# Row maxima half a unit ahead, and both batches as one row of units

## The chip, the cores and the metric

The kernel runs on one core of a Trainium2 chip. The metric is the device time of one execution in microseconds (us). Three runs of the kernel before took 4086.3, 4100.18 and 4105.85 us; the median is 4100.18.

The engines are named as in the profile: PE is TensorE (PEld its weight loads), DVE is VectorE, ACT is ScalarE, POOL is GpSimd, SP is SyncE, which issues the transfers.

## What is computed

One layer: attention with one key and value head for 32 query heads, ALiBi bias and causal mask, then layer norm, then a feed-forward product with a routed low-rank part, and a second norm. x is 2 x 2048 x 1024 in float32.

```python
q = (x @ Wq).reshape(b, s, 32, 32)
k, v = x @ Wkv          # one head of 32 each
scores = einsum('bqhd,bkd->bhqk', q, k) * scale + slopes * (kpos - qpos)
attn = softmax(where(causal, scores, -inf), axis=-1)
x = layernorm(x + einsum('bhqk,bkd->bqhd', attn, v) @ Wo)
x = layernorm(x + x @ W.T + b + lora_of_chosen_rank(x))
```

## The kernel before

Attention is written for 2 batches, each of 4 segments of 512 queries. A segment s has 8 units, each of 4 heads (64 units in all, numbered 0 to 63 here; units 0 to 7 are segment 0 of the first batch). A unit takes its 512 queries against 4(s+1) key tiles of 128. Its steps:

- X (once a segment): the 512 rows of x are turned by TensorE in 8 parts (`turn_x`, line 652), split into a high part by ScalarE (`split_x`, line 454) and a low part by VectorE (line 542). KV: projection of keys and values, 24 products into ps_m, taken by VectorE (`take_kv`, lines 550 to 556). VT: the values are turned (line 673).
- Q: 8 parts of three products (lines 656 to 658) into ps_m for the unit after next; QE: taken from there head by head by ScalarE and VectorE (`take_q`, lines 466 and 567). WS: the next weights, loaded by SP into wq_raw, are split by ScalarE and POOL (lines 459 and 418).
- A: one chunk of scores, 128 queries against up to 512 keys, for the row maximum alone: TensorE into one of the three banks ps_a (line 692, with the mask 695), maximum by VectorE (line 574). The next unit has 16(s+1) of them.
- CV and CT: VectorE reduces the maxima (line 579), forms the shift (line 581), TensorE turns it into ps_m (line 700), VectorE copies it (line 585) and SP writes it into the last row of the query stack, where the next unit's first S waits for it.
- S: the scores of one key tile and one head, 128 keys by 512 queries, into one of two banks ps_s (line 756, mask 759), and the exponential by ScalarE (line 494). Such an S is a slot; a unit has 16(s+1) slots, four to a key tile.
- PV: probabilities times values of one key tile, SM: the same with ones for the row sums (line 779, four heads at a time, two passes each). In segments 1 to 3 POOL adds the probabilities of two tiles (ADD, line 437) and one SP takes the sum of both. OE: ScalarE copies both results; R: reciprocals by VectorE in 4 parts (line 592), the product by POOL (line 444), then the store.

`plan_step` writes the order of a unit's slots out for every engine: S, then what is put in that slot. Chunks A of unit g+1 go evenly into all but the last 7 slots (6 in segment 0); CV follows, CT two slots later. X, KV, VT, Q and QE follow one another from slot 1 on; X, KV and VT stand in the last unit but one of a segment. WS comes behind QE, in segment 0 in the last slot. PV and SM or SP go behind the second score of the next key tile. Every step waits on counting semaphores; a chunk A waits for the maximum three chunks before it.

`walk` runs each batch on its own: a prologue (X, KV, VT, Q, A for the first unit, Q for the second) in front of segment 0, then the units. SP loads wkv, then at 13 us x and wq_raw. The turned x goes into ps_m, one bank, save in the prologue (two banks of ps_a). The feed-forward stage begins when all of attention is through.

## Time and profile before

| | us |
|---|---|
| median of three runs | 4100.18 |
| the profiled execution's own time | 4086.85 |
| its span, first to last instruction | 4085.0 |
| attention, to the end of unit 63 | 3178.4 |
| feed-forward stage | 906.6 |
| PE busy in the span | 3766.8 (92%) |
| DVE, ACT, POOL busy | 2474.2 (61%), 1925.0 (47%), 1360.6 (33%) |
| PE's mean granted clock, of full | 0.959 |

Busy time counts an instruction from start to end. PE's matmuls are pipelined and their ends are modelled, so a busy PE may also be waiting. A unit is measured here from its first S to the next unit's first S. A wait in the timeline is shown in brackets: idle time of the engine, and what ended it.

### The profile page before, as it was taken

Reading aid. Unit: us, or ns where it says so; the run is one execution under the profiler, and the core shown is the slowest. Engines: PE = TensorE matmul, PEld = TensorE weight load, DVE = VectorE, ACT = ScalarE, POOL = GpSimd, SP = SyncE. Lnnn points to the kernel's source line nnn. Section 1 sums busy time; section 2 is a strip of 40 time slices with the busy share of each in tenths; the row PEclk is TensorE's granted clock in tenths of the full one; section 3 lists DMA queues with packets and bytes.
Section 4 is the critical chain, followed back from the end, with each engine's and each line's share of the span. In section 5 each row is a group of like instructions: output and inputs, shape, how many; then the busy total and the mean of one; then the engine's idle time right before and its main releaser. Section 6 shows DMA issues by size and latency. Waiting matters only on the chain. (4 is left out here: it accounts for less than half of the span.)

```text
span 4085.0 us, 56649 instructions
## 1 busy us (share of the span) xinstructions
PE 3766.8 (92%) x22065; PEld 2354.1 (58%) x22065; DVE 2474.2 (61%) x4462; ACT 1925.0 (47%) x3253; POOL 1360.6 (33%) x420
## 2 busy tenths in 40 slices
PE   5989989999999997888999999999998599999998
PEld 3555555555454543555555554544443488888887
DVE  4557767776767672555776777676764344444444
ACT  2435655665666664344665666566666211111110
POOL 1113434444445453112433444455555100000000
PEclk8879999999999998888999999999999799999999
DMA  2111110000000001211111000000000412111111
GB/s 71 40 53 32 32 42 22 22 22 22 14 19 14 19 6 34 60 37 45 32 30 45 19 22 22 14 22 13 20 14 3 145 62 62 61 57 57 57 60 52
DMA packets 158918, 150.73 MB, mean 37 GB/s; under 512 B 8388, under 2 KB 141508, under 8 KB 156584
## 3 DMA queue, kind: packets, MB, share of 16 engines
q1 hardware_dynamic: 158696, 147.70, 12.4%
q8 instruction: 148, 2.42, 0.2%
q14 instruction: 74, 0.61, 0.0%
HBM read 96.75 MB, written 33.62 MB: 32 GB/s over the span
## 5 line engine op out<-in xcount | busy, mean ns | idle before, releaser
L494 ACT ACTIVATE prob<-ps_s,alibi 128x512 f32<-128x512 f32 (+3 forms) x2560 | 1521.6, 623 | 1110.5 <-PE ps_s L756 545.6
L574 DVE TENSOR_REDUCE mxp<-ps_a 128x1 f32<-128x512 f32 (+3 forms) x2560 | 1457.8, 605 | 800.7 <-PE ps_a L695 418.4
L437 POOL TENSOR_TENSOR prob<-prob 128x2048 f32<-128x2048 f32 (+1 forms) x240 | 1044.4, 4351 | 1126.5 <-ACT prob L494 1126.5
L756 PE MATMUL ps_s<-qst,kexp 97*128 97x512 f32 (+3 forms) x2560 | 1092.3, 437 | 74.5 <-ACT prob L494 55.1
L692 PE MATMUL ps_a<-kmax,qst 97*128 97x512 f32 (+3 forms) x2560 | 956.1, 399 | 34.3 <-DVE mxp L574 17.3
L756 PEld LDWEIGHTS ps_s<-qst,kexp 97*128 97x128 f32 x2560 | 492.3, 194 | 727.6 <-ACT prob L494 425.1
L779 PE MATMUL ps_o<-prob,val 128*32 128x512 f32 (+3 forms) x5120 | 612.2, 551 | 7.7 <-ACT prob L494 7.7
L692 PEld LDWEIGHTS ps_a<-kmax,qst 97*128 97x128 f32 x2560 | 504.3, 198 | 116.7 <-DVE mxp L574 59.5
L779 PE MATMUL ps_sum<-prob,ones 128*32 128x512 f32 (+3 forms) x3200 | 361.4, 525 | 0.0
L965 POOL TENSOR_TENSOR hb_sb<-h_sb,bias_b 128x1024 f32<-128x1024 f32 x32 | 76.8, 2401 | 791.9 <-DVE z_sb L1109 732.2
L592 DVE RECIPROCAL r_sb<-s_sb 128x128 f32<-128x128 f32 x256 | 233.4, 928 | 113.8 <-ACT s_sb L500 113.1
L995 ACT ACTIVATE root<-var 128x1 f32<-128x1 f32 x64 | 13.0, 203 | 604.6 <-DVE var L1054 604.6
L418 POOL TENSOR_TENSOR wql<-wq_raw,wqh 128x1024 fp32r<-128x1024 f32 x65 | 154.4, 2375 | 396.3 <-ACT wqh L459 390.1
L1166 PE MATMUL ps_z<-wth,hth 128*128 128x364 f32 x768 | 254.8, 332 | 5.3 <-DVE htl L1121 5.3
L1168 PE MATMUL ps_z<-wtl,hth 128*128 128x364 f32 x768 | 252.9, 329 | 0.0
L1170 PE MATMUL ps_z<-wth,htl 128*128 128x364 f32 x768 | 252.8, 329 | 0.0
L695 PE MATMUL ps_a<-maskb,identb 128*128 128x128 bf16 x1024 | 242.5, 238 | 0.0
L759 PE MATMUL ps_s<-maskt,identb 128*128 128x128 bf16 x1024 | 239.6, 238 | 0.0
L656 PE MATMUL ps_m<-xh,wqh 128*128 128x512 f32 x512 | 225.1, 440 | 6.9 <-POOL wql L418 4.7
L567 DVE SCALAR_TENSOR_TENSOR qst<-ps_m,qst 32x512 fp32r<-32x512 f32 x256 | 176.1, 688 | 80.7 <-ACT qst L466 76.7
L657 PE MATMUL ps_m<-xl,wqh 128*128 128x512 f32 x512 | 213.8, 418 | 0.0
L658 PE MATMUL ps_m<-xh,wql 128*128 128x512 f32 x512 | 211.9, 414 | 0.0
(148 smaller groups left out, 3709.3 us busy)
## 6 DMA issues: line engine op xcount, KB each, us to landing
wq_raw<-in_L_attn_Wq SPq DMA_DIRECT2D x65, 512.0 KB, 4.0
xs<-in_L_attn_hidden_states SPq DMA_DIRECT2D x9, 2048.0 KB, 8.7
qst<-qst SPq DMA_DIRECT2D x64, 256.0 KB
att_scratch<-at_sb SPq DMA_DIRECT2D x64, 256.0 KB, 2.4
at_raw<-att_scratch SPq DMA_DIRECT2D x32, 512.0 KB, 5.3
x_sb<-in_L_attn_hidden_states SPq DMA_DIRECT2D x32, 512.0 KB, 4.3
out<-z_sb SPq DMA_DIRECT2D x32, 512.0 KB, 3.2
z_sb<-in_L_attn_Wo SPq DMA_DIRECT2D x4, 512.0 KB, 5.1
```

The source lines that it names most:

```text
L437: nc.gpsimd.tensor_tensor(even[:, :, c1:], even[:, :, c1:], odd[:, :, c1:], ALU.add).then_inc(pair_done, 1)
L494: nc.scalar.activation(prob[slot][:, h, c0:], ps_s[bank][:, c0:], ACT.Exp, bias=alibi_of(u, h, k - QT * s)).then_inc(e_done, 1)
L574: nc.vector.tensor_reduce(mxp[:, h * QT + t, c:c + 1], ps_a[bank][:, 0:cols], AX.X, ALU.max).then_inc(a_done, 1)
L592: nc.vector.reciprocal(r_sb[:, cols], s_sb[:, cols]).then_inc(r_done, 1)
L692: last = nc.tensor.matmul(ps[:, 0:cols], qst[buf][0:KR, h, t * P:(t + 1) * P], kmax[0:KR, c * QB:c * QB + cols], start=True, stop=c < s)
L695: last = nc.tensor.matmul(ps[:, cols - P:cols], identb[:], maskb[:], start=False, stop=True)
L756: last = nc.tensor.matmul(ps_s[bank][:, c0:], kexp[0:KR, k * P:(k + 1) * P], qst[buf][0:KR, h, c0:], start=True, stop=not diagonal)
L759: last = nc.tensor.matmul(ps_s[bank][:, c0:c0 + P], identb[:], maskt[:], start=False, stop=True)
L779: last = nc.tensor.matmul(ps[h * DH:(h + 1) * DH, c0:], weights, prob[slot][:, h, c0:], start=k == 0, stop=k == ktiles(s) - 1)
L1166: nc.tensor.matmul(ps, hth[:, c], wth[:, c, piece(p)], start=c == 0, stop=False, skip_group_check=True)
L1168: nc.tensor.matmul(ps, hth[:, c], wtl[:, c, piece(p)], start=False, stop=False, skip_group_check=True)
L1170: last = nc.tensor.matmul(ps, htl[:, c], wth[:, c, piece(p)], start=False, stop=False, skip_group_check=True)
```

## The change

The 64 units of both batches are one row; there is no second prologue. Keys and values stand in a ring of five segments, so that the first segment of the second batch can be prepared while the first batch still runs. The position row of kmax is written for each segment by VectorE.

The chunks A for unit g+1 end about halfway through unit g (A_END), CV follows at once and CT some slots later (CT_AT); in the rest of unit g stand the first chunks of unit g+2 (8, 13, 23 or 27 of them, none where unit g+2 has only 16). X, KV and VT go into the third unit from a segment's end. Each step has a table of places by segment.

The three banks ps_a are one ring: chunks, turned x and the turned maxima all take the next bank, and the counter a_done counts all three. The maxima themselves are turned, and VectorE makes the shift from the turned ones in one operation with a table `base` that is computed at the start. The shift operation of line 581 is gone.

In segments 2 and 3 the row sums (SM, SP) go behind the fourth score of a key tile (SM_AT), PV behind the second. WS in segment 0 is at slot 5. SP loads x first, then the weights; ScalarE waits for the bias table only before its first exponential.

The core of the diff ("..." marks what is left out):

```diff
--- before.py
+++ after.py
...
+SEGS = B * NSEG
+UNITS = SEGS * HG
+RING = NSEG + 1
...
+def ring(sg):
+    return sg % RING * QB
+def key_tile(g, k):
+    return (seg_of(g) // NSEG * NSEG + k // QT) % RING * QT + k % QT
...
-Q_SPACE = 0.5
-X_SPACE = (1, 1.5, 2.5, 2.5)
-RECIP_AT = ((2, 4, 6, 8, 9), (5, 19, 28, 29, 30), (14, 26, 44, 45, 46), (20, 36, 60, 61, 62))
...
+CHUNKS_AHEAD = (8, 13, 23, 27)
+A_END = (9, 17, 25, 33)
+A_FROM = (11, 18, 26, 34)
+Q_AT = ((0, 0.5), (0, 1), (0, 1.25), (1, 1.5))
+QE_AT = ((3, 1), (7, 2), (9, 3), (11, 5))
+CT_AT = (11, 18, 30, 38)
+X_AT = ((7, 0.5), (9, 1.25), (19, 2), (22, 3))
+KV_AT = (11, 25, 35, 46)
+VT_AT = (17, 27, 40, 47)
+PV_AT = (1, 1, 1, 1)
+SM_AT = (1, 1, 3, 3)
+WS_AT = (5, 17, 27, 33)
+RECIP_AT = ((0, 2, 3, 8, 11), (6, 16, 25, 29, 30), (22, 27, 44, 45, 46), (20, 36, 60, 61, 62))
+def chunks_ahead(g):
+    if g < 2:
+        return 0
+    return min(CHUNKS_AHEAD[seg_of(g - 2) % NSEG], len(a_chunks(g)) - GH * QT)
+def prepares(g):
+    return g % HG == HG - 3 and seg_of(g) + 1 < SEGS
...
+def plan_unit(g):
+    s = seg_of(g) % NSEG
+    n = ktiles(g)
     slots = n * GH
-    chunks = a_chunks(sa) if has_a else []
-    a_slots = slots - (7 if s else 6)
     at = {}
-    for i, x in enumerate(chunks):
-        at.setdefault(i * a_slots // len(chunks), []).append(("A", x))
-    if has_a:
-        at.setdefault(a_slots, []).append(("CV", 0))
-        at.setdefault(a_slots + 2, []).append(("CT", 0))
-    space = X_SPACE[s]
-    misc = [(space, ("X", j)) for j in range(DC)] + [(1, ("KV", 0)), (space, ("VT", 0))] if prep else []
-    if has_q:
-        misc += [(1 if s else Q_SPACE, ("Q", j)) for j in range(DC)]
-        misc += [(min(s + 1, 3), ("QE", h)) for h in range(GH)]
-    place = 1.0
-    for width, x in misc:
-        at.setdefault(min(a_slots - 1, int(place)), []).append(x)
-        place += width
-    if has_q:
-        at.setdefault(min(a_slots - 1, int(place)) if s else slots - 1, []).append(("WS", 0))
+    def put(slot, what, arg):
+        at.setdefault(min(slots - 1, int(slot)), []).append((what, arg))
+    if g + 1 < UNITS:
+        first = chunks_ahead(g + 1)
+        rest = a_chunks(g + 1)[first:]
+        for i, x in enumerate(rest):
+            put(i * A_END[s] / len(rest), "A", (g + 1, first + i, x))
+        put(A_END[s], "CV", 0)
+    if g + 2 < UNITS:
+        for j in range(DC):
+            put(Q_AT[s][0] + j * Q_AT[s][1], "Q", j)
+        for h in range(GH):
+            put(QE_AT[s][0] + h * QE_AT[s][1], "QE", h)
+    if g + 3 < UNITS:
+        put(WS_AT[s], "WS", 0)
+    if g + 1 < UNITS:
+        put(CT_AT[s], "CT", 0)
+    if prepares(g):
+        for j in range(DC):
+            put(X_AT[s][0] + j * X_AT[s][1], "X", j)
+        put(KV_AT[s], "KV", 0)
+        put(VT_AT[s], "VT", 0)
+    if g + 2 < UNITS:
+        ahead = a_chunks(g + 2)[:chunks_ahead(g + 2)]
+        for i, x in enumerate(ahead):
+            put(A_FROM[s] + i * (slots - A_FROM[s]) / len(ahead), "A", (g + 2, i, x))
...
+            if k and h == PV_AT[s]:
                 out.append(("PV", k - 1))
-                if k > 2 * summed:
-                    out.append(("SM", k - 1))
-                if k >= 4 and k % 2 == 0 and k // 2 - 2 < summed:
-                    out.append(("SP", k // 2 - 2))
+            if k > 2 * summed and h == SM_AT[s]:
+                out.append(("SM", k - 1))
+            if k >= 4 and k % 2 == 0 and k // 2 - 2 < summed and h == SM_AT[s]:
+                out.append(("SP", k // 2 - 2))
...
-        def turned_in(s, j):
-            return ps_m if s else ps_a[j % 2]
...
+            sp.dma_start(xs[:], xb[0]).then_inc(x_in, 16)
             sp.dma_start(wkv_raw[:], wkv.rearrange("(c p) m -> p c m", p=P)).then_inc(wkv_in, 16)
-            sp.wait_ge(vec_c, 2 * NH + 3 + 2 * QT)
+            sp.dma_start(wq_raw[:], wq_v[0]).then_inc(wq_in, 16)
...
+            def prologue():
+                for g in range(2):
+                    put_slopes(g)
+                    load_wq(g + 1)
+                    repeat_q(g)
+                load_x(1, DC)
+                put_shift(0, FIRST - 1)
+            def step(g, plan, count):
+                if g + 2 < UNITS:
+                    put_slopes(g + 2)
+                if g + 3 < UNITS:
+                    load_wq(g + 3)
                 for what, arg in plan:
                     if what == "R" and arg == QT:
-                        store_before(unit_no(b, s, u))
+                        store(g - 1)
                     if what == "QE" and arg == GH - 1:
-                        repeat_q(b, s2, u2, parity(s, const + 2))
+                        repeat_q(g + 2)
                     if what == "CT":
-                        s1, u1 = ahead(s, u, 1, const)
-                        put_shift(b, s1, u1, parity(s, const + 1))
-            def epilogue(b):
-                load_x(b, NSEG, (b + 1) % B)
-                store_before(b * UB + UB)
-            sp.dma_start(xs[:], xb[0, 0]).then_inc(x_in, 16)
-            sp.dma_start(wq_raw[:], wq_v[0]).then_inc(wq_in, 16)
-            walk(sp, prologue, step, epilogue)
-            sp.wait_ge(wq_in, START + 16 * (B * UB + 1))
-            sp.wait_ge(at_out, START + 16 * B * UB)
-            sp.wait_ge(x_in, START + 16 * (B * NSEG + 1))
+                        put_shift(g + 1, count)
+                    if what in ("A", "CT", "X"):
+                        count += 1
+                    if what == "X" and arg == DC - 1 and seg_of(g) + 2 < SEGS:
+                        load_x(seg_of(g) + 2, count)
...
+                nc.vector.tensor_scalar(kmax[3 * DH:KR, cols], kpos[3 * DH:KR], float(QB * sg), None,
+                                        ALU.add).then_inc(kv_lo, 1)
...
+            def maximum(count, g, i, chunk):
                 h, t, c, cols = chunk
-                dve.wait_ge(a_full, tiles + (i + 1))
-                nc.vector.tensor_reduce(mxp[:, h * QT + t, c:c + 1], ps_a[bank][:, 0:cols], AX.X,
+                if i == 0:
+                    dve.wait_ge(c_max, START + g)
+                dve.wait_ge(a_full, START + count + 1)
+                nc.vector.tensor_reduce(mxp[:, h * QT + t, c:c + 1], ps_a[bank_of(count)][:, 0:cols], AX.X,
...
+            def reduce_max(g, count):
+                s = seg_of(g) % NSEG
+                dve.wait_ge(a_done, START + count)
                 nc.vector.tensor_reduce(mx[:], mxp[:, :, 0:s + 1], AX.X, ALU.max).then_inc(c_max, 1)
-                dve.wait_ge(c_max, START + g + 1)
-                nc.vector.scalar_tensor_tensor(shift[:], slope4_c[:, bass.ds(u * (GH * QT), GH * QT)], float(QB * s),
-                                               mx[:], ALU.mult, ALU.subtract).then_inc(c_vec, 1)
-                dve.wait_ge(c_ps, START + g + 1)
+            def shifts(g, count):
+                sg, u = seg_of(g), g % HG
+                dve.wait_ge(a_full, START + count + 1)
                 dve.wait_ge(c_in, START + 16 * g)
-                nc.vector.tensor_copy(shift_t[:], ps_m[0:GH * QT, 0:P]).then_inc(c_out, 1)
-            def divide(g, part):
+                nc.vector.tensor_scalar(shift_t[:], ps_a[bank_of(count)][0:GH * QT, 0:P], -1.0, base[:, sg, u:u + 1],
+                                        ALU.mult, ALU.add).then_inc(a_done, 1)
...
+            def turn_x(sg, j, count):
                 if j == 0:
                     pe.wait_ge(x_in, START + 16 * (sg + 1))
-                    pe.wait_ge(c_out, START + g)
-                if s == 0:
-                    if j == 0:
-                        pe.wait_ge(a_done, START + b * TILES_B)
-                    elif j > 1:
-                        pe.wait_ge(xl_done, START + DC * sg + j - 1)
-                elif j:
-                    pe.wait_ge(xl_done, START + DC * sg + j)
+                pe.wait_ge(a_done, START + max(0, count - 2))
                 for t in range(QT):
-                    last = nc.tensor.transpose(turned_in(s, j)[:, t * P:(t + 1) * P], xs[:, t, j * P:(j + 1) * P], ident[:])
-                last.then_inc(xt_ps, 1)
+                    last = nc.tensor.transpose(ps_a[bank_of(count)][:, t * P:(t + 1) * P],
+                                               xs[:, t, j * P:(j + 1) * P], ident[:])
+                last.then_inc(a_full, 1)
...
+            def turn_max(g, count):
+                pe.wait_ge(c_max, START + g + 1)
+                pe.wait_ge(a_done, START + count - 2)
+                nc.tensor.transpose(ps_a[bank_of(count)][0:GH * QT, 0:P], mx[:], ident[:]).then_inc(a_full, 1)
...
+                        pe.wait_ge(ql_done, START + GH * min(UNITS, g + 3))
+                        project_kv(seg_of(g) + 1, turned)
...
+                        if arg == 0 and prepares(g - 1):
+                            pe.wait_ge(vt_done, START + seg_of(g) + 2)
                         elif arg == 0:
-                            pe.wait_ge(c_out, START + g + 1)
+                            pe.wait_ge(ql_done, START + GH * (g + 2))
```

## Rows read from the trace of the kernel before

**Rows 1.** Busy time by stage: stretch, its length, each engine's busy time, clock
```profile
core 0: us, PE busy (x) PEld busy (x) DVE busy (x) ACT busy (x) POOL busy (x), PEclk, DMA share, GB/s
0.00:80.46 80.46, 36.02 (x142) 26.41 (x143) 33.71 (x123) 13.50 (x20) 11.92 (x18) 0.86 0.19 57
80.46:320.96 240.50, 213.93 (x1301) 135.38 (x1301) 128.66 (x241) 102.10 (x190) 25.45 (x14) 0.84 0.18 53
320.96:638.53 317.57, 298.30 (x1880) 173.09 (x1876) 226.71 (x373) 186.44 (x321) 132.17 (x41) 0.97 0.12 34
638.53:1076.20 437.67, 415.69 (x2525) 222.39 (x2517) 310.30 (x501) 268.45 (x448) 202.91 (x57) 0.99 0.08 20
1076.20:1598.03 521.83, 495.14 (x2955) 239.49 (x2951) 329.34 (x525) 340.66 (x559) 271.61 (x71) 1.00 0.06 15
1598.03:1660.68 62.65, 35.38 (x142) 25.98 (x142) 27.23 (x44) 12.47 (x20) 5.94 (x3) 0.73 0.20 63
```
**Rows 2.** The same for single units: 1, 2, 6, 9, 15, 17, 22, 27, 31
```profile
105.85:130.31 24.46, 21.25 (x158) 13.30 (x154) 14.41 (x27) 12.49 (x24) 3.69 (x3) 0.97 0.18 45
130.31:157.48 27.17, 24.92 (x157) 15.46 (x153) 14.54 (x27) 12.49 (x23) 3.63 (x3) 0.81 0.16 40
239.11:287.26 48.15, 38.35 (x218) 26.32 (x214) 21.34 (x40) 16.51 (x31) 3.64 (x3) 0.82 0.09 23
359.20:394.47 35.27, 34.22 (x230) 19.95 (x226) 26.35 (x43) 22.72 (x39) 16.25 (x6) 1.00 0.13 31
593.49:638.59 45.10, 42.71 (x245) 23.60 (x241) 35.41 (x59) 23.11 (x39) 16.18 (x5) 0.92 0.19 64
690.53:742.55 52.02, 49.71 (x310) 26.39 (x306) 36.90 (x59) 33.04 (x55) 25.37 (x8) 1.00 0.08 22
950.59:1015.87 65.28, 60.92 (x370) 34.66 (x366) 43.04 (x72) 36.58 (x63) 25.34 (x8) 0.97 0.07 17
1277.37:1344.37 67.00, 64.56 (x390) 32.47 (x386) 47.02 (x75) 43.56 (x71) 34.58 (x10) 1.00 0.06 17
1540.44:1598.03 57.59, 47.98 (x284) 17.00 (x280) 3.39 (x4) 39.31 (x67) 32.18 (x9) 1.00 0.04 11
```
**Rows 3.** Unit 27: eight slots' window, then timeline: start, length, engine, instruction, idle before
```profile
1304.17:1312.23 8.06, 7.90 (x42) 3.37 (x42) 5.80 (x10) 5.17 (x9) 6.25 (x2) 1.00 0.00 0
...
1313.04 0.39 PE L756 MATMUL ps_s<-qst,kexp 97*128 97x512 f32 x1
1313.28 0.39 PE L692 MATMUL ps_a<-kmax,qst 97*128 97x512 f32 x1
1313.59 1.06 PE L779 MATMUL ps_o<-prob,val 128*32 128x512 f32 x8
1314.48 1.04 PE L779 MATMUL ps_sum<-prob,ones 128*32 128x512 f32 x8
1315.45 0.50 PE L756 MATMUL ps_s<-qst,kexp 97*128 97x512 f32 x1
1315.79 0.40 PE L692 MATMUL ps_a<-kmax,qst 97*128 97x512 f32 x1
...
1315.99 2.54 ACT L494 ACTIVATE prob<-ps_s,alibi 128x512 f32<-128x512 f32 x4 [1.83 <-PE ps_s L756]
```
**Rows 4.** Instructions grouped by line and shape: busy, mean ns, idle before, releasers
```profile
L494 ACT ACTIVATE prob<-ps_s,alibi 128x512 f32<-128x512 f32 x1792 | 1177.1, 687 | 750.3 <-PE ps_s L756 545.6 <-PE ps_s L759 195.7
```
**Rows 5.** Shift operation (ns min/median/max, first and last start); waits of CT and of Q
```profile
L581 DVE SCALAR_TENSOR_TENSOR shift<-slope,mx x64: 174/2217/2251, 75.7 to 3114.9; 128x16 f32<-128x16 f32 x64
...
1340.89 0.27 PE L700 MATMUL ps_m<-ident,shift 128*16 128x128 f32 x1 [0.87 <-DVE shift L581]
...
108.76 0.47 PE L656 MATMUL ps_m<-xh,wqh 128*128 128x512 f32 x1 [0.89 <-POOL wql L418]
```
**Rows 6.** Timeline of unit 22: VectorE's part of x, weight loads of the next x turned
```profile
953.01 0.69 DVE L542 TENSOR_TENSOR xl<-ps_m,xh 128x512 fp32r<-128x512 f32 x1 [0.34 <-ACT xh L454]
...
953.75 0.42 PEld L652 LDWEIGHTS ps_m<-ident,xs 128*128 128x128 f32 x4 [0.92 <-DVE xl L542]
```
**Rows 7.** Timeline of the start, ScalarE
```profile
22.41 1.28 ACT L459 ACT_TABLE_LOAD   x1 [22.41 <-DMA wq_raw<-in_L_attn_Wq]
```

457 lines of the change are left out of this document (207 added, 250 removed).

## The prediction

> **What bounds the kernel now.** I read the stretches by stage first [rows 1], then single units [rows 2], then some slots of a segment-3 unit instruction by instruction [rows 3]. Busy shares come first, the clock beside them next, starts of instructions last. Attention ends at 3178 us of the 4085 us span; the feed-forward stage behind it is not touched, so it keeps its 907 us. TensorE is the busiest engine in every segment [rows 1] (214 of 240.5 us, 298 of 317.6, 416 of 437.7, 495 of 521.8), and VectorE and ScalarE are busy 42% to 71% of them. The second batch's segments repeat these within 0.2 us, so each stands once. Two stretches are of another kind: the first 80.5 us, and the 62.7 us at 1598, where the second batch starts from nothing and only 35 us of TensorE work lie. The clock is the second thing to see: full in the later segments (0.97 to 1.00), 0.84 in segment 0 [rows 1], where single units show 0.81 and 27.2 us against 0.97 and 24.5 us for the same work [rows 2]. It fell there between its two levels, 2.4 and 1.2 GHz, after the thin end of a unit: no score chunk is left, 128-wide scores alternate with their exponentials, and the shift transpose waits.
>
> Busy time of TensorE hides stalls, since a matmul's end is modelled. So I take start to start. In [rows 3] a 512-wide score goes S to A in 0.24 us, A to the probability products in 0.31, these take 0.89 and then 0.97 up to the next S, and that S takes 0.34 instead of 0.24: a matmul of 512 is 0.23, and each burst of probability products costs 0.88 a product and 0.29 for going in and out. While it runs ScalarE has at most two score banks to work on and then idles 1.83 us; afterwards it is TensorE that waits, because an exponential takes 0.69 [rows 4] and S plus A only 0.46. Eight slots (two key tiles, with 9 chunks, two PV bursts, one of them with SP behind it) take 8.06 us [rows 3]; the sum of the parts is 17 x 0.23 + 3 x 0.88 + 2 x 0.29 = 7.1. So a bit over 0.9 us in 8 is stall that the 92% busy doesn't show. The same sum over a whole unit gives (Q 5.5, full chunks and scores 0.23 each, the 32 diagonal ones 8.7 together, PV and sums, 0.29 a burst, CT 0.3) about 20, 33, 46.8 and 60.5 us for segments 0 to 3, where the units take 27.2, 35.3, 52.0 and 67.0 [rows 2].
>
> **The change, part by part.**
> Shift chain (all 64 units). Before, CV, the shift operation and CT stand in the last 7 slots, and TensorE waits 0.87 us at CT for the shift operation [rows 5]. Now CT is 2 to 5 slots behind CV, with chunks and scores between, and that operation is gone. I take 1.05 us a unit from segment 1 on (wait and the slot's latency). The operation itself lasts 2.22 us in the median and 0.17 at the least [rows 5], always with pool's pair sum beside it where it is long. Its replacement reads PSUM; nearest row is the 0.28 us copy that it replaces, and between 0.28 and 2.2 it would still be behind other work. By "GPSIMD Engine Reference" of the Trainium skill, section Specifications, GpSimd's SBUF interfaces are shared with VectorE and contend with two-input instructions; the 2.22 against 0.17 us agrees, and the rule speaks against the new one-row addition into kmax, eight times; at 2 us each that would be 16 us at most, and nothing hangs on it.
>
> Bursts split, in segments 2 and 3 (SM_AT 3). Each SP goes two slots behind PV. It adds 0.29 us a split burst, and takes most stalls: following eight slots with exponentials of 0.69 and two banks I get 7.7 us for 8.06. Both ends: 7.4 (no stall left) and 8.35 (no stall removed, 0.29 added). Five such pairs in a segment-3 unit, three in segment 2: 1.75 and 1.05 us. Where no chunks fill the slots, as in the last unit (57.6 us, ScalarE sets it [rows 2]), splitting brings nothing and may cost 0.5.
>
> Chunks in all slots, Q spread over 12 slots instead of 8 (segment 3). It fills slots in which TensorE waited for ScalarE: 0.3 (segment 3), 0.5 (segment 2), 0.3 (segment 1). New units: **64.0, 49.4 and 34.0 us** for 67.0, 52.0 and 35.3.
>
> Segment 0. WS moves from the last slot to slot 5, so Q need not wait for wql (0.89 us [rows 5]); CT leaves the thin end (1.2 us); take_q goes earlier. Adding the slots up with the tail's ping-pong of small exponentials: 22.1 us at full clock against 24.5. Whether the clock stays up isn't told by any row: the thin end shrinks from 7 to about 5 us but is still there. A fall costs 2.7 us now (27.2 less 24.5 [rows 2]); I charge half of it, 1.3: **23.4 us** (22.1 to 25).
>
> Preparing a segment. The turned x takes banks of the ring of three instead of one bank, so its TensorE work is 8 x 0.42 = 3.4 [rows 6], KV 24 x 0.23 = 5.5, the transposed values 0.5: 9.4 us. A ring entry of x waits for ScalarE's copy, behind up to two exponentials, and VectorE's subtraction of 0.69 [rows 6], and the maxima queued behind it on VectorE wait too, and with them TensorE two entries on. I charge 5.5, 5, 3 and 4 us of stall for segments 0 to 3 (in the last VT follows KV by one slot, while take_kv lasts about 3 us). Before it cost 21 us in segment 0 and 13 in segment 2 [rows 2]. Chunks that the next segment has more: 16 x 0.23 = 3.7, with up to 5 us while VectorE is full (it is busy 35.4 of 45.1 us in such a unit now [rows 2]).
>
> Start. x is issued ahead of the weights at 3 us instead of 13, and wq_raw, for which ScalarE waits until 22.4 [rows 7], comes about 9.6 us earlier; three banks for turned x save some 2.5: 12 us. SP's new order holds nothing back: put_slopes and load_wq wait for things of the unit before, and store stands ahead of put_shift only in segment 0, where the division of the unit before is done by slot 10 or 11; if it isn't, the next unit's first score waits for it. Load_x is issued a segment early.
>
> The second start (62.7 us) goes: its work of 9.4 us is a preparation in unit 29, and chunks and Q for segment 4 stand in units 30 and 31, in which ScalarE has room. Units 30 and 31: 62 us each; 62 and 63: 59.5 and 58.
>
> **The sum**, in the profiled execution:
> - start: 12 less.
> - segment 0: 24.5 + 4 x 23.4 + 38.3 + 26.2 + 29.1 = 211.7 for 240.5; the second time one less: 59 less in both.
> - segment 1: 6 x 34.0 + 48.4 + 42.5 = 295 for 317.6, twice: 45 less.
> - segment 2: 6 x 49.4 + 61.8 + 55.1 = 413 for 437.7, twice: 49 less.
> - segment 3: 5 x 64.0 + 77.4 + 62 + 62 = 521 for 521.8 + 62.7, so 63 less; then 6 x 64.0 + 59.5 + 58 = 501.5 for 521.9, 20 less.
> That is 248 us: a span of 3837, 3839 as the execution's own time (4086.85 for a span of 4085.0). The median of the three runs, 4100.18, lies 13 us above that execution; I add half: **3845 us**.
>
> **Rivals.**
> Only the serial waits go. The start, the second start and the CT waits vanish, but TensorE's ring and banks keep their stalls (split bursts bring nothing: 16 x 1.95, 16 x 1.5 and 16 x 0.2 us back) and segment 0 falls to the low clock in every unit as now (24 us): 3845 + 82 = 3927. For it: the chunk stream still runs through three banks, and a burst still outlasts two exponentials. Against: the 8 slots of [rows 3] have idle time on both engines in turn, which is what an even order cures. The Trainium skill's "TensorE: Matmul & The Clock Gate", section "A second HAM failure mode: psum-queue depth-cycling", tells of a clock that goes up and down while TensorE idles briefly between groups on cycling PSUM banks; the 0.81 of segment 0's units agrees, and by that rule it would stay.
> More goes. Clock full in segment 0 (21 us) and no stall in preparations (31 us): 3793. For it: 40 to 50 of these 52 us are my charges, not rows.
> Slower. Chunks of two units, turned x and turned maxima all go through one ring and one in-order VectorE queue. If at each R, QE and CV (10 in a unit) a maximum of 0.69 us comes late and TensorE loses it, that is 6.9 x 64 = 442 us: 4287. It decides once VectorE's work plus its waits for ScalarE fill a unit; now it is busy 47 of 67, 26 of 35 and 14.5 of 27 us [rows 2], so it should not, save in the units 7, 15 and 23.
> The change doesn't do what it says: x first gains nothing if ScalarE still waits for wq_raw, its third transfer. That would be 9 us, within my range.
>
> **Chances.** Forecast 0.57, only the serial waits 0.20, more 0.16, VectorE's queue 0.04, other 0.03. The range takes in the better case (3793) and the serial-waits case (3927) with some us for the span's own spread: 3785 to 3935. A measurement of this kernel can tell about 0.5%, 20 us. Faster by over that: 0.94; within: 0.02; slower: 0.04.
>
> **What would show it.** Units (first S to first S) of 64, 49.4, 34 and 22 to 23.5 us; no gap at 1550 to 1600; TensorE's wait at the turned maxima under 0.2 us; eight slots in segment 3 at 7.7 us; clock of segment 0 at 0.9 or more; the first score at about 68 us; VectorE's maxima waiting less on TensorE. It is wrong if a segment-3 unit is over 66 us (the burst reasoning fails), if segment 0 still shows 27 us (the clock), or if TensorE's waits on mxp or xl grow beyond some 100 us (the ring).

## The result, and the profile after

The changed kernel takes **3815.8 us** (median of 4 runs, 3811.5 to 3819.8), the kernel before 4095.1 (4 runs): ratio 0.932, 95% interval 0.929 to 0.934. The profiled execution took 3819.8 us for a span of 3818.0, against the forecast of 3839 for that kind of number and 3845 for the median.

Engines and clock on the page of the changed kernel (busy us, share of the span; clock in 40 slices):

```profile
PE 3660.5 (96%) x22081; PEld 2255.5 (59%) x22081; DVE 2362.7 (62%) x4414; ACT 1929.4 (51%) x3252; POOL 1357.6 (36%) x419
...
PEclk8999999999999999999999999999997999999999
```

Its busy time by stage, with the columns of [rows 1]: start, segments 0 to 3, segment 4 (segment 0 of the second batch), segment 7, feed-forward. Attention ends where ScalarE starts its last copy of a result, as in the kernel before:

```profile
0.00:71.50 71.50, 35.50 (x158) 26.83 (x158) 32.33 (x131) 13.39 (x20) 9.64 (x18) 0.83 0.31 99
71.50:270.00 198.50, 185.97 (x1309) 118.59 (x1309) 129.11 (x242) 101.86 (x190) 27.89 (x15) 0.97 0.18 51
270.00:563.60 293.60, 287.33 (x1886) 162.78 (x1882) 212.03 (x372) 188.94 (x320) 130.02 (x40) 1.00 0.13 36
563.60:978.20 414.60, 412.61 (x2531) 213.98 (x2527) 300.07 (x504) 271.20 (x448) 203.40 (x56) 1.00 0.10 27
978.20:1503.10 524.90, 512.17 (x3074) 249.68 (x3070) 323.75 (x535) 349.69 (x576) 276.24 (x72) 0.99 0.08 21
1503.10:1696.60 193.50, 181.52 (x1313) 115.52 (x1309) 132.22 (x246) 102.81 (x192) 29.17 (x16) 1.00 0.20 56
...
2404.70:2910.40 505.70, 496.05 (x2932) 230.19 (x2928) 298.05 (x495) 337.63 (x557) 269.34 (x69) 0.98 0.05 14
2910.40:3818.00 907.60, 849.53 (x4496) 761.31 (x4496) 423.04 (x1015) 103.72 (x181) 78.44 (x37) 0.96 0.21 66
```

The 62.7 us stage of [rows 1] has no counterpart, and segment 0's clock is 0.97 and 1.00 where it was 0.84. Single units, which answer to [rows 2]: 3, 5 (prepares), 11, 19, 27, 29 (prepares), 63:

```profile
140.63:162.06 21.43, 20.63 (x153) 12.94 (x153) 13.33 (x26) 11.33 (x21) 3.64 (x2) 1.00 0.12 33
183.47:217.61 34.14, 30.28 (x217) 20.98 (x213) 21.83 (x40) 16.27 (x31) 3.64 (x2) 1.00 0.31 99
374.48:409.01 34.53, 34.04 (x229) 18.69 (x225) 23.87 (x42) 23.12 (x39) 16.26 (x5) 1.00 0.13 32
714.97:764.60 49.63, 49.48 (x310) 25.07 (x306) 34.62 (x58) 33.29 (x55) 25.41 (x7) 1.00 0.09 23
1173.33:1238.03 64.70, 64.31 (x389) 31.40 (x385) 44.65 (x74) 43.28 (x71) 34.59 (x9) 1.00 0.07 17
1302.75:1385.32 82.57, 75.70 (x450) 40.41 (x446) 56.35 (x88) 47.60 (x79) 34.50 (x9) 0.96 0.12 39
2850.54:2910.41 59.87, 54.73 (x284) 18.32 (x280) 3.39 (x4) 39.24 (x67) 32.01 (x8) 0.83 0.02 6
```

Where the 267 us between the two spans lie, from the starts of units in both traces (minus is time saved):

| part | forecast, us | measured, us |
|---|---|---|
| start | -12 | -8.9 |
| segment 0, both times | -59 | -89.3 |
| segment 1, both times | -45 | -48.0 |
| segment 2, both times | -49 | -46.0 |
| segment 3 and the second start | -63 | -59.6 |
| segment 3, second time | -20 | -16.2 |
| feed-forward | 0 | +1.0 |
| sum | -248 | -267.0 |

So six of seven terms fell within 4 us, and segment 0 gave 30 us more than the sum said. That the six came so close is in part luck, since misses inside them cancel. In segment 1 the six steady units took 4 us more than forecast, while the preparing unit took 2.8 and the one before the next segment 2.6 us less.

### The profile page after: what moved, and what is told of

Read it like the earlier page. It is cut to its first block and busy times, and to the rows that moved or that the text cites. A ratio compares the mean times of both kernels' runs of the same rounds, so it can differ in the third digit from the quotient of the medians.

```text
span 3818.0 us, 56682 instructions
## 1 busy us (share of the span) xinstructions
PE 3660.5 (96%) x22081; PEld 2255.5 (59%) x22081; DVE 2362.7 (62%) x4414; ACT 1929.4 (51%) x3252; POOL 1357.6 (36%) x419
## 5 line engine op out<-in xcount | busy, mean ns | idle before, releaser
L771 PE MATMUL ps_s<-qst,kexp 97*128 97x512 f32 (+3 forms) x2560 | 1071.5, 424 | 34.9 <-ACT prob L507 17.0
L702 PE MATMUL ps_a<-kmax,qst 97*128 97x512 f32 (+3 forms) x2560 | 969.8, 397 | 21.0 <-DVE mxp L585 8.8
L716 PE MATMUL ps_o<-prob,val 128*32 128x512 f32 (+3 forms) x5120 | 603.2, 543 | 6.0 <-ACT prob L507 6.0
L716 PE MATMUL ps_sum<-prob,ones 128*32 128x512 f32 (+3 forms) x3200 | 344.6, 510 | 0.0
L668 PE MATMUL ps_m<-xh,wqh 128*128 128x512 f32 x512 | 217.3, 425 | 0.4 <-DVE val L570 0.4
L1162 PE MATMUL ps_y<-woh,ath 128*128 128x512 f32 x512 | 206.5, 403 | 3.9 <-DVE atl L1046 3.9
L670 PE MATMUL ps_m<-xh,wql 128*128 128x512 f32 x512 | 204.0, 399 | 0.0
```

Of the source, the lines that this page charges most:

```text
L702: last = nc.tensor.matmul(ps[:, 0:cols], qst[buf][0:KR, h, t * P:(t + 1) * P], kmax[0:KR, ring(sg):ring(sg) + cols], start=True, stop=sg < ...
L716: last = nc.tensor.matmul(ps[h * DH:(h + 1) * DH, c0:], weights, prob[slot_of(steps_before(g) + k)][:, h, c0:], start=k == 0, stop=k == kt ...
L771: last = nc.tensor.matmul(bank[:, c0:], kexp[0:KR, at:at + P], qst[g % 3][0:KR, h, c0:], start=True, stop=not diagonal)
L1162: nc.tensor.matmul(ps, ath[par][:, c], woh[:, c, cols], start=first, stop=False)
```

## The experiments

Each edit is to the changed kernel, 3816 us, save one that says so. A unit is measured from first score to first score, as before.

**Do split bursts help?** First the split taken back, then carried on into segment 1.

```diff
-SM_AT = (1, 1, 3, 3)
+SM_AT = (1, 1, 1, 1)
```

> Change undone: in segments 2 and 3 each sum over a pair of key tiles again follows the probability products in the same slot. Theory (a joined burst outlasts two banks of scores, so ScalarE and then TensorE idle): 0.35 us more per joined burst, five in a segment-3 unit and three in a segment-2 unit, 16 units each: 28 + 17 = 45 us more than the changed kernel, 3861 us; a steady segment-3 unit at 66.4 us, a segment-2 unit at 50.7 us. Rival (entering and leaving a burst is what costs): 0.29 us less each, 8 x 16 x 0.29 = 37 us less, 3779 us, units at 63.3 and 48.8 us.

Measured: 3861.9 us (3854 to 3870), 46 more. A steady segment-3 unit is 66.1 us, 1.4 more, a segment-2 unit 50.2, 0.56 more. Where few chunks are left the price is higher: unit 30 takes 64.1 instead of 60.3. Unit 27 and unit 30 of this run:

```profile
1181.61:1247.68 66.07, 64.47 (x389) 32.07 (x385) 44.49 (x75) 43.48 (x71) 34.55 (x10) 1.00 0.07 17
1398.94:1463.05 64.11, 59.48 (x363) 28.60 (x359) 27.83 (x48) 43.16 (x71) 34.85 (x10) 1.00 0.08 21
```

TensorE's busy time in unit 27 is the same as with split bursts (64.3 and 64.5), yet the unit is 1.4 us longer: that is the stall. The theory holds (46 us for its 45), with a bit less in a steady unit (0.28 and 0.19 us a burst where I had 0.35) and more in the units without a full stream of chunks. Eight slots tell the same: between slots 28 and 48 of unit 27 they take 8.0 to 8.1 us in the kernel before, 7.5 to 7.6 in the changed kernel (the forecast was 7.7) and 7.7 to 8.3 here. The eight from slot 24 on, the window of [rows 3], take 8.0 in the changed kernel, hardly less.

```diff
-SM_AT = (1, 1, 3, 3)
+SM_AT = (1, 3, 3, 3)
```

> One step further: the sums are split from the products in segment 1 too (two pairs inside a unit, and one single tile's sum). Theory that splitting pays wherever chunks fill the slots: 0.35 us less for each of two, 16 units: 11 us less, 3805 us, unit 33.8 us instead of 34.5. Rival (a segment-1 unit at 34.5 us is only 1.5 us above the sum of its parts, so no stall is left to take, and each more burst costs 0.29 us): 3 x 0.29 x 16 = 14 us more, 3830 us, unit 35.4 us.

Measured: 3830.6 us (3823 to 3837), 15 more, a segment-1 unit 35.1 instead of 34.5. The rival holds (14 more forecast): in segment 1 splitting doesn't pay. Why not is argued, from the order of the slots. A segment-1 unit has as many chunks for each score as one of segment 3, but Q and the diagonal matmuls lie on half as many scores. TensorE has hardly a stall left for the split to take, and each burst more costs its way in and out.

**Would a third bank of scores be the better cure?**

```diff
-        ps_s = [pb(ctx, f"ps_s{i}", [P, QB]) for i in range(2)]
-        ps_a = [pb(ctx, f"ps_a{i}", [P, QB]) for i in range(3)]
+        ps_s = [pb(ctx, f"ps_s{i}", [P, QB]) for i in range(3)]
+        ps_a = [pb(ctx, f"ps_a{i}", [P, QB]) for i in range(2)]
...
```

The waits for a free bank are changed to the new numbers with it.

> One PSUM bank goes from the ring of chunks, turned x and turned maxima (two instead of three) to the scores (three instead of two). Theory of the prediction (a burst of probability products outlasts two banks of scores, and that is the stall left in segments 2 and 3, about 2.5 us of a 64.7 us unit): with three banks ScalarE idles less behind a burst, units of 62.5 and 48.5 us, some 40 us less, 3775 us. Rival (the stream of chunks is then the tight one: each maximum takes 0.69 us on an in-order engine and two banks leave no slack when it is late): TensorE's waits for the maxima go over 200 us, units 67 us or more, 3860 us or more.

Measured: 3996.9 us (3996 to 4004), 181 more. TensorE's weight loads for chunks wait for the maxima for 207 us, 24 in the changed kernel:

```profile
PEld ps_a L703 <- DVE mxp L586: 207.0, 456, 2.1
```

A steady segment-3 unit is 66.3 us, a segment-1 unit 36.5, a preparing unit in segment 1 55.2 instead of 45.7. The rival holds: with two banks the ring of chunks binds in every segment. It doesn't refute the theory on the scores, since a bank was taken away as another was given. Where there are no chunks it fares well: the last unit takes 50.2 us here, and 53.1 with two banks of scores and split bursts at full clock.

**What holds segment 0's clock up?** Three edits, each of which moves work that TensorE waits for.

```diff
-WS_AT = (5, 17, 27, 33)
+WS_AT = (15, 17, 27, 33)
```

> The split of the next projection weights goes back to the last slot of a segment-0 unit, so the projection of Q, in the first slot, waits for wql again: some 0.9 us a unit, in 12 or so units, 11 us. Theory 1 (that wait together with the thin end is what let the clock fall before): granted clock about 0.8 in segment 0 again, 2.7 us a unit more, 11 + 32 = 43 us more, 3859 us, units near 25 us. Theory 2 (the thin end with the waiting turned maxima made it fall, not this wait): clock stays at 0.97 or more, 11 us more, 3827 us, units 22.3 us.

Measured: 3869.6 us (3867 to 3873), 54 more. Waits of TensorE in units 1 to 6 (in total, times, longest), and the window of unit 4:

```profile
PE ps_m L668 <- POOL wql L427: 8.3, 5, 1.9
...
172.79:198.90 26.11, 23.52 (x157) 14.75 (x153) 13.86 (x26) 12.28 (x24) 3.63 (x2) 0.87 0.16 42
```

The wait is 1.9 us, not 0.9, and in each unit that has it the clock is down to 1.2 GHz for 3.4 to 6.8 us (0.87 to 0.94 in the mean): 26.1 us for 21.4 in unit 4. Theory 1 has it right in the main, 54 us for its 43: a wait of that size in unit after unit is enough. But it is not the one that the kernel before had: its trace shows the wait for wql once in segment 0 of each batch [rows 5].

```diff
-CHUNKS_AHEAD = (8, 13, 23, 27)
-A_END = (9, 17, 25, 33)
+CHUNKS_AHEAD = (0, 0, 0, 0)
+A_END = (10, 25, 41, 57)
...
-CT_AT = (11, 18, 30, 38)
+CT_AT = (12, 27, 43, 59)
```

> No chunks half a unit ahead: the maxima of the next unit end 7 slots before its start (6 in segment 0) and are turned two slots later, as before; all else is the changed kernel's (maxima turned without the shift operation, ring of banks, split bursts). Theory (the lead is what fills the last slots and hides the latency from the last maximum to the turned ones): 0.9 us a unit in segments 1 to 3, 48 units, 43 us; segment 0 gets the thin end back and the low clock with it, 1.2 + 2.7 us a unit in 14 units, 55 us; together about 98 us more, 3914 us. Rival (the removed shift operation was the whole gain, the lead only moves chunks): within 10 us of the changed kernel, clock of segment 0 full, unit lengths 64.7, 49.6, 34.5 and 21.4 us.

Measured: 3872.0 us (3866 to 3876), 56 more, between the two. Units 4, 11, 19 and 27 of this run:

```profile
162.83:184.69 21.86, 20.68 (x153) 12.99 (x154) 13.70 (x26) 12.08 (x23) 3.64 (x2) 1.00 0.18 50
383.50:418.73 35.23, 34.49 (x230) 20.00 (x226) 24.22 (x42) 22.93 (x39) 16.20 (x5) 1.00 0.12 31
732.92:782.74 49.82, 49.57 (x310) 25.96 (x306) 34.49 (x58) 32.98 (x55) 25.46 (x7) 1.00 0.09 23
1194.75:1259.51 64.76, 64.28 (x390) 32.07 (x386) 44.77 (x74) 43.45 (x71) 34.57 (x9) 1.00 0.07 17
```

Both theories fail. Steady units of segments 0 to 3 lose only 0.45, 0.70, 0.19 and 0.06 us without the lead. What it is worth lies where a segment ends: units 7, 15, 23 and 30 take 33.7, 46.3, 57.8 and 64.7 us for 27.2, 39.9, 54.2 and 60.3. By the plans units 7, 15 and 23 hold as many chunks in both kernels (32, 48 and 64), but without the lead all of them must be done before the last 6 or 7 slots, where with it 8, 13 or 23 of them stand in the second half. Unit 30 holds 64 chunks for 37, because nothing was done ahead. And segment 0 has its thin end back, with full clock: the thin end alone doesn't bring the clock down.

```diff
-CT_AT = (11, 18, 30, 38)
+CT_AT = (14, 18, 30, 38)
```

> Turned maxima of a segment-0 unit in slot 14 of 16 instead of 11, so that the next unit's first score waits longer for their copy and its transfer. By the changed kernel's trace that wait is 1.8 us in such a unit; three slots of 0.7 to 0.9 us later it should be 4.0 us. Theory 1 (the clock fell in the kernel before because TensorE stood still or nearly so for some microseconds in each unit, whatever the cause): it falls again here, units 26 to 27 us, 14 units, 70 us more. Theory 2 (a wait of that size doesn't do it, it was the wait for the low part of the projection weights with the thin end together): clock full, units 23.6 us, 31 us more, 3847 us.

Measured: 3836.6 us (2 runs), 21 more, neither of the two. The wait at a unit's start is 1.0 us (once 1.5), not 4.0: the 1.8 us that I started from stand at the start of one unit only (see the three small moves below). Units 3, 4 and 34 to 36 take 24.0 us, with the clock down for 3.4 us in each; units 1, 2 and 33, with the same wait of 1.0 us, keep full clock and take 22.5 to 23.0. Unit 4:

```profile
165.90:189.90 24.00, 22.10 (x153) 14.10 (x154) 13.88 (x26) 12.41 (x24) 3.64 (x2) 0.93 0.17 45
```

**What was the removed shift operation worth?** In the kernel without the lead, a stand-in was put back. Its value is that of mx, and TensorE waits for it and turns it in place of mx:

```diff
+                nc.vector.scalar_tensor_tensor(shift[:], mx[:], 1.0, mx[:], ALU.mult, ALU.min).then_inc(c_vec, 1)
```

> The kernel without the lead of half a unit (measured at 3872 us) with a stand-in for the removed shift operation put back: 128x16, two operands in SBUF, between the column maxima and their turning, which waits for it. Theory (behind GpSimd's pair sum it takes about 2.2 us and TensorE waits 0.87 us for it at a place where no chunk is left): 0.8 us a unit in segments 1 to 3, 48 units, about 38 us more, 3910 us; a segment-3 unit 65.5 us, segment-0 units unchanged at 21.9 us since it is short there. Rival (the wait is hidden by the scores around it): within 10 us.

Measured: 3978.8 us (2 runs), 107 more than the 3872.0 without it, nearly three times the theory. Segment-0 units are unchanged (21.9 us, full clock), segment-1 units 35.5, 0.3 more, with a wait of 0.8 us at the turned maxima. In segments 2 and 3 TensorE waits 1.6 us in each unit. Where the clock stays full the unit is 1.8 us longer (51.6 and 66.6 us), and where it falls behind that wait 3.3 to 5.0 us (up to 54.6 and 69.8): part of the 107 us is the clock's. Unit 26: the stand-in on VectorE, the pair sum on GpSimd, and TensorE's turned maxima:

```profile
1214.30 2.21 DVE L595 SCALAR_TENSOR_TENSOR shift<-mx 128x16 f32<-128x16 f32 x1
...
1213.04 3.44 POOL L454 TENSOR_TENSOR prob<-prob 128x1536 f32<-128x1536 f32 x1 [3.99 <-ACT prob L509]
...
1216.57 0.28 PE L715 MATMUL ps_a<-ident,shift 128*16 128x128 f32 x1 [1.62 <-DVE shift L595]
```

The operation ends at 1216.51, the pair sum at 1216.48. It doesn't take 2.2 us, it waits until GpSimd is done, and how long that is depends on where in the pair sum it falls. The kernel before shows the same of its own operation. Unit 27:

```profile
1338.53 2.22 DVE L581 SCALAR_TENSOR_TENSOR shift<-slope,mx 128x16 f32<-128x16 f32 x1
...
1337.26 3.45 POOL L437 TENSOR_TENSOR prob<-prob 128x1536 f32<-128x1536 f32 x1 [3.79 <-ACT prob L494]
```

Wherever it took over 1 us there, it ended 0.03 to 0.04 us behind a GpSimd instruction, a pair sum or, four times, the split of the weights.

**Which operations wait so?** Three small ones, A, B and C, that nobody reads, behind the maxima of each unit but the first, in an order that rotates.

```diff
+nc.vector.tensor_tensor(side[0][:], mx[:], slope[:, 0:GH * QT], ALU.subtract)          # A
+nc.vector.tensor_scalar(side[1][:], mx[:], 2.0, None, ALU.mult)                         # B
+nc.vector.tensor_tensor(side[2][0:P // 2], mx[0:P // 2], slope[0:P // 2, 0:GH * QT], ALU.subtract)  # C
```

> The changed kernel with three small operations more on VectorE behind each unit's column maxima, 128x16, in an order that rotates from unit to unit, and nobody reads them: A subtracts two operands in SBUF on 128 partitions, B scales one operand in SBUF by a constant, C is A on 64 partitions. Theory (two operands in SBUF go through an interface that GpSimd holds during its pair sum, whatever their size): A and C 0.17 to 0.3 us in the units of segment 0, where no pair sum runs, and about 2 us in the median in segments 2 and 3; B 0.1 to 0.3 us everywhere. Rival 1 (it is the place right behind the maxima that is slow, not the operands): whichever is first in the rotation takes 2 us, B too. Rival 2 (size matters, a 16-wide operation slips in between): A and C near 0.3 us everywhere, and the 2.2 us of the old shift operation were its own. Time: the changed kernel's within 10 us.

Measured: 4079 us (one run), 263 more. VectorE and GpSimd in unit 26:

```profile
1253.22 0.22 DVE L593 TENSOR_REDUCE mx<-mxp 128x16 f32<-128x64 f32 x1
1253.48 3.40 DVE L601 TENSOR_TENSOR side<-mx,slope 128x16 f32<-128x16 f32 x1
1256.80 2.37 DVE L603 TENSOR_SCALAR side<-mx 128x16 f32<-128x16 f32 x1
1259.08 0.16 DVE L605 TENSOR_TENSOR side<-mx,slope 64x16 f32<-64x16 f32 x1
...
1252.25 4.58 POOL L454 TENSOR_TENSOR prob<-prob 128x2048 f32<-128x2048 f32 x1 [3.46 <-ACT prob L509]
1256.79 2.34 POOL L429 TENSOR_TENSOR wql<-wq_raw,wqh 128x1024 fp32r<-128x1024 f32 x1
```

The first of the three ends with the pair sum (1256.88 and 1256.83), the second with the split of the weights behind it (1259.17 and 1259.13), the third finds GpSimd idle and takes 0.16 us. In the units with another order B is first and is held just as long (the first of the three takes 3.3 to 3.4 us in the median of segments 1 to 3, whichever it is), so one operand in SBUF is enough. The theory was wrong on B, and rival 1 has the times right: whichever comes first is slow. Its reason isn't, for the place is slow only while GpSimd works. The reduction of 128x16, also from SBUF to SBUF and in the middle of the same pair sum, takes 0.22 us. The Trainium skill's "SBUF — State Buffer", section "Who interferes with whom", says just this: a VectorE operation with two inputs in SBUF, or a copy, cast or tensor_scalar from SBUF to SBUF in a mode with two ports, and a GpSimd operation lock each other out for the whole instruction, and a reduction never takes part. The rows agree for VectorE held by GpSimd; the other way round isn't shown.

My time for it, within 10 us, was far out. In segment 0 (no pair sums) the steady units stay at 21.4 us. In segment 3 they take 66.2 to 72.3: 5.8 us on VectorE in one piece leave TensorE waiting for the ring (3.1 us at once), and then its clock falls (0.93 in unit 26). Where no chunk is queued behind them the held operations cost nothing: unit 30 has 10.4 us of them and takes 60.3 us, as in the changed kernel. Unit 26, its longest wait and its window:

```profile
PE ps_a L717 <- DVE mxp L587: 3.1, 1, 3.1
...
1218.27:1290.33 72.06, 68.54 (x389) 33.12 (x385) 50.64 (x77) 43.61 (x71) 34.48 (x9) 0.93 0.06 16
```

**Unit 29**, which prepares segment 4, took 82.6 us where I had 77.4. VectorE, GpSimd and TensorE in the changed kernel:

```profile
1361.44 3.84 DVE L562 TENSOR_SCALAR kmax<-kpos 1x512 fp32r<-1x512 f32 x1
1365.32 0.42 DVE L565 CAST kmax<-kexp 96x512 fp32r<-96x512 f32 x1
...
1360.51 4.49 POOL L452 TENSOR_TENSOR prob<-prob 128x2048 f32<-128x2048 f32 x1 [8.88 <-ACT prob L507]
...
1365.89 0.60 PE L683 MATMUL ps_m<-ident,vt_sb 32*128 32x32 f32 x4 [6.18 <-DVE kmax L565]
```

The new one-row addition, 0.42 us in the other seven preparations, takes 3.84 here and ends 0.28 us behind the pair sum. Two edits were to show that, beside another one at the start of the kernel:

```diff
-            sp.dma_start(xs[:], xb[0]).then_inc(x_in, 16)
             sp.dma_start(wkv_raw[:], wkv.rearrange("(c p) m -> p c m", p=P)).then_inc(wkv_in, 16)
-            sp.dma_start(wq_raw[:], wq_v[0]).then_inc(wq_in, 16)
...
             sp.wait_ge(rows_out, 16)
+            sp.dma_start(xs[:], xb[0]).then_inc(x_in, 16)
+            sp.dma_start(wq_raw[:], wq_v[0]).then_inc(wq_in, 16)
...
             dve.wait_ge(kv_ps, START + sg + 1)
+            nc.vector.tensor_scalar(kmax[3 * DH:KR, cols], kpos[3 * DH:KR], float(QB * sg), None, ALU.add)
             nc.vector.tensor_copy(kexp[0:3 * DH, cols], ps_m[0:3 * DH]).then_inc(kv_hi, 1)
...
-            nc.vector.tensor_scalar(kmax[3 * DH:KR, cols], kpos[3 * DH:KR], float(QB * sg), None, ALU.add)
```

> Two edits far apart in time. (1) x and the first projection weights are loaded behind the slope rows again. Theory of the prediction (x first is worth 9.6 us, the three banks 2.5): first score 9.6 us later, at 81 us. Rival (the start is set by something else, since the whole gain there was 8.9 us and not 12): less than 5 us later. (2) The one-row addition into kmax stands ahead of the copies out of PSUM instead of behind them; in unit 29 it took 3.84 us instead of 0.42, beside GpSimd's pair sum. Theory A (only the form of that operation is held by the pair sum, and ahead of the copies it is done before the sum starts): TensorE's wait at the turned values falls from 6.2 to about 2.8 us, unit 29 to 79 us. Theory B (any operation from SBUF to SBUF is held, other than reductions): the copy of the keys from kexp to kmax is caught in its place, 3.3 us long, and the wait stays within 0.6 us of 6.2.

Measured: 3822.0 us (2 runs). The first score comes at 80.2 us, 8.6 later than in the profiled run of the changed kernel (other profiled executions with the same start have it at 70.7 to 73.2), so on the start the theory holds. In unit 29 VectorE and GpSimd read:

```profile
1367.62 0.42 DVE L557 TENSOR_SCALAR kmax<-kpos 1x512 fp32r<-1x512 f32 x1 [6.06 <-PE ps_m L670]
...
1370.24 3.39 DVE L565 CAST kmax<-kexp 96x512 fp32r<-96x512 f32 x1
...
1368.85 4.50 POOL L452 TENSOR_TENSOR prob<-prob 128x2048 f32<-128x2048 f32 x1 [8.89 <-ACT prob L507]
```

Theory B holds: the row is quick before the pair sum starts, and the copy of the keys, SBUF to SBUF, is caught instead. TensorE waits 5.7 us, and the unit takes 84.6. Of the three reads of PSUM between them the last two are beside the pair sum too, and keep their 0.70 and 0.68 us.

**Is there a better plan?** The changed kernel again, and two versions of it.

> The changed kernel itself, beside the two that follow: 3810 to 3820 us. Its profiled execution showed the low clock for 20 us in the last unit of attention (57.9 us), while an experiment with the same last unit showed full clock there (51.1 us). Theory (a unit with no chunks left is near the edge, and executions differ): single executions spread over some 7 us, and the profiled one here has the last unit either at 51 or at 57 to 58 us, nothing between.

Measured: 3815.6 us (5 runs, 3807 to 3817), ratio 0.931 (0.930 to 0.933). The last unit, up to the last copy, takes 53.1 us here at full clock, for 59.9 at 0.83 above: the same instructions, 6.7 us apart between two executions (the 51.1 and 57.9 of the expectation stop 2 us earlier).

```diff
-CT_AT = (11, 18, 30, 38)
-VT_AT = (17, 27, 40, 47)
+CT_AT = (10, 18, 30, 38)
+VT_AT = (17, 27, 40, 54)
...
+    sm = SM_AT[s] if g + 1 < UNITS else 1
...
```

(`sm` then takes the place of SM_AT[s] in the plan.)

> Three moves in the plan: in segment 3 the values are turned seven slots later in a preparing unit; in segment 0 the maxima are turned one slot earlier; in the last unit the sums go with the products again. Theory: unit 29 loses TensorE's wait of 6.2 us for the key copies and goes from 82.6 to 76.5 us; in segment 0 the wait of 1.8 us for the shift's transfer at a unit's start shrinks by one slot, 0.8 us, in 14 units, 11 us; last unit 2 us; together 19 us less than the changed kernel. Rival (waits only move: the maxima of segment 0 come right behind the last column maximum and TensorE waits for them there, and unit 29 stalls for ScalarE instead): within 6 us of the changed kernel.

Measured: 3820.3 us (5 runs, 3818 to 3821), ratio 0.933 (0.932 to 0.934): nothing gained. Unit 29 takes 83.5 us:

```profile
1360.83 3.86 DVE L563 TENSOR_SCALAR kmax<-kpos 1x512 fp32r<-1x512 f32 x1
...
1365.93 0.80 PE L703 MATMUL ps_a<-kmax,qst 97*128 97x512 f32 x1 [5.48 <-DVE mxp L586]
```

The rival holds on the time (within 6 us), and waits did only move. With the turned values out of the way TensorE waits 5.5 us for a maximum that is queued behind the same held operation. The last unit takes 57.5 us with the sums joined, 53.1 split, both at full clock: I had chosen the joined form because of the long last unit above, which was the clock's, and the prediction's "may cost 0.5" for the split there has the wrong sign too. In segment 0 a steady unit grows from 21.4 to 21.9 us, with a wait of 0.39 us at the turned maxima. The 1.8 us that I meant to save stood at the start of unit 3 alone (1.3 at unit 34), and I had taken it for all. There the shift's transfer stands in SP's queue right behind the store of the unit before and takes 4.4 us to land, 1.8 to 2.1 in the other steady units of this segment. With CT one slot earlier it stands ahead of that store, lands in 1.8 us, and both waits are gone.

```diff
-A_END = (9, 17, 25, 33)
-CT_AT = (11, 18, 30, 38)
+A_END = (8, 17, 25, 33)
+CT_AT = (9, 18, 30, 38)
```

(The other two moves stay as in the run before.)

> As the one before, and in segment 0 the remaining chunks end in slot 8 instead of 9, and the maxima are turned in slot 9. Theory: the whole 1.8 us wait at a unit's start goes, units of 20 us, 14 x 1.4 = 20 us, with the other two moves 28 us less than the changed kernel. Rival (VectorE is full in these slots, with four reads of Q, a reciprocal and the maxima in line, so the chunks wait for it): a segment-0 unit at 21.4 us or more, no gain over the kernel before it.

Measured: 3896.1 us (5 runs, 3877 to 3905), 80 more. TensorE waits 1.7 us at the turned maxima in every steady segment-0 unit, and the rival holds. In units 1, 33, 34 and 35 the clock stays full all the same, and they take 24.2 us; in units 2, 3, 4, 32 and 36 it falls, and they take 25.7 to 30.7. Units 1 and 3:

```profile
100.10:124.26 24.16, 20.90 (x158) 13.00 (x154) 13.70 (x26) 12.28 (x23) 3.65 (x2) 1.00 0.16 45
...
150.98:181.52 30.54, 27.56 (x157) 16.37 (x153) 13.79 (x26) 12.46 (x23) 3.64 (x2) 0.72 0.13 35
```

None of the versions beats the changed kernel.

## Why the prediction was right, and where it was off

**Steady units.** 64.7, 49.6 and 34.5 us for a forecast of 64.0, 49.4 and 34.0. The step "bursts split" was sound in kind and 0.3 to 0.5 us a unit too large (1.4 for 1.75, 0.56 for 1.05). For the last unit it was wrong: split bursts bring 4.4 us there.

The step "shift chain" had about the right size in segment 3, and for a reason that I hadn't seen. I called the operation's 2.2 us its duration under contention; it is the rest of GpSimd's instruction. The prediction also has it always beside the pair sum, where four times it was the weights' split. What is left of the gain in a segment-3 unit is 2.3 - 1.4 (split) - 0.06 (lead) = 0.84 us, where I had put 1.05. That fits the wait of 0.87 at CT [rows 5], but it is a sum and no test, and elsewhere the sum doesn't fit: the wait at CT was 0.86 us in segments 1 and 2 too, and there 2.4 - 0.56 - 0.19 = 1.6 us are left in segment 2 and nothing in segment 1 (35.27 before, 35.23 without the lead). The 0.7 us of segment 1 came from the lead, where I had counted 1.3 in all. What the operation costs was measured in the kernel without the lead alone: 0.3 us a unit in segment 1, 1.8 and more in segments 2 and 3.

**Segment 0** is the term that failed: 23.4 us a unit, made of 22.1 and half of a fall of the clock, against 21.4 measured at full clock. The charge of 1.3 us was for not knowing, and the 22.1 was 0.7 too high. Of the 30 us, 15 lie in units 0 to 4 and 32 to 36, 8 in the preparing units 5 and 37, and 7 in the two units behind each. The step's reason was wrong as well. I blamed the thin end, and the kernel without the lead has a thin end and full clock in its steady units, also with the shift operation put back. What the runs show is that falls go with a standstill of TensorE that comes back in unit after unit: 1.2 us at CT before, in each of units 1 to 5, 1.9 at wql, 1.0 at the unit's start, 1.7 at the maxima turned too early. In the kernel without the lead, with no wait over 0.5 us in a steady unit, none fell. The length doesn't settle it: with 0.7 us (three banks of scores) two steady units of nine fell, with 1.7 us four kept full clock and five fell, and in the changed kernel a single wait of 1.8 us, at the start of unit 3, left the clock full. What else decides stays open. TensorE's waits in units 0 to 5 of the kernel before (total, times, longest):

```profile
PE ps_m L700 <- DVE shift L581: 6.4, 6, 1.2
```

Unit 0 has 0.2 of them, the other five 1.2 each. In segment 0 that operation takes 0.17 us, so the wait was for VectorE's line ahead of it, in which reads of Q still stood between the last maxima; the changed plan takes Q earlier. That it is this move which empties the line is argued from the order of the two traces; it wasn't tried alone. Of the rival "only the serial waits go" the part on segment 0 fell with it: by the rule that it cites, of the Trainium skill's "TensorE: Matmul & The Clock Gate", the 0.81 would have stayed, and the changed kernel shows 1.00 there, still with banks in turn. The rival "more goes" had this part right (21 us of its 52).

**Preparing units** took 34.1, 45.7, 60.1 and 82.6 us for 38.3, 48.4, 61.8 and 77.4. Over its steady unit and 9.4 us of work each stalled 3.3, 1.7, 1.1 and 8.5 us, where I had charged 5.5, 5, 3 and 4. For the last one the prediction had the place right (VT one slot behind KV) and the price wrong. It spoke against the one-row addition itself, by a rule on two inputs that doesn't reach an operation with one, put 2 us on each, and added that nothing hangs on it. One of eight was caught, for 3.4 us, and both TensorE and the maxima hung on it, and the clock fell for 6.8 us.

**The start** gave 8.9 for 12. The two parts are as said: ScalarE starts its first split at 13.4 instead of 23.7 us, and from there to the first copy of Q it is 26.6 instead of 29.5 us. That alone is 13 us. But from the last copy of Q in the prologue to the first score it now is 12.9 us, 8.5 before, and here the step "SP's new order holds nothing back" failed. The maxima are turned sooner (3.7 us behind that copy, 6.0 before), but SP issues the next segment's x, 2 MB, just ahead of the first shift's transfer, which then takes 8.2 us to land and not 1.8:

```profile
62.73 0.58 SPq L352 DMA_DIRECT2D xs<-in_L_attn_hidden_states  x1
63.35 0.72 SPq L371 DMA_DIRECT2D qst<-shift_t  x1
...
62.41 0.38 PE L711 MATMUL ps_a<-ident,mx 128*16 128x128 f32 x1 [3.77 <-DVE mx L591]
71.55 0.79 PE L771 MATMUL ps_s<-qst,kexp 97*128 97x512 f32 x1 [8.76 <-DMA qst<-shift_t]
```

The difference of the two landings, 6.4 us, is my estimate of what the other order would bring; it wasn't tried. The same step had feared that a store ahead of the shift's transfer makes a first score wait in segment 0, and that came: 1.8 us at unit 3, 1.3 at unit 34.

With x late again ScalarE's first split comes 8.9 us later and the first score 8.6, for the 9.6 forecast.

**The second start** went as forecast: 59.6 for 63. Units 24 to 28 together took 4.6 us more than said and unit 29 5.2, units 30 and 31 6.3 less (60.3 and 57.5 for 62 each), so here too misses cancel.

**The spread.** The forecast's 6 us between span and median wasn't needed: the profiled execution here lies 4 us above the median, not below, and 6.7 us hang on the clock in the last unit, which has no chunks left. In the profiled executions with the same last unit it stayed full in some (53.1 us) and fell in others (57.5 to 59.9).

**What would show it.** As the prediction put it: no gap at 1550 to 1600, steady units, clock of segment 0 over 0.9, TensorE's wait at the turned maxima 0.14 us or none, maxima waiting less (VectorE waited 577 us in all for chunks, 778 before). Eight slots in segment 3 came out at 7.5 for 7.7, but at 8.0 in the window of [rows 3]. First score at 68 us was wrong (71.6).

## What to carry to other kernels

Before an operation of GpSimd is set beside a chain on VectorE, look at which VectorE operations in that chain go from SBUF to SBUF: each was held here until GpSimd's instruction ended, however small it was, and with it everything that was queued behind it. The 0.17 us that the shift operation takes by itself say nothing of its cost: its stand-in cost 107 us in the whole kernel. And a split pays only where the other engine waits for the burst: the same split gained 46 us in segments 2 and 3 and lost 15 in segment 1. Last, look at what stands ahead of a small transfer on which a chain hangs: behind 2 MB it took 8.2 us for 1.8.
